# A linear-attention kernel: keys are turned before the scores, and the context products follow the scores directly

## What is computed

```python
qkv = x @ Wqkv + bqkv
xn = x / max(norm(x), 1e-12)                  # each head of q and of k
feat = exp(clip(proj(xn) * sqrt_2s - s, -20, 20)) * weights
kv_cur = cumsum(k_ch * v_ch, axis=2) + kv_state   # a chunk of 128
k_cur = cumsum(k_ch, axis=2) + k_state
ctx = einsum('bhtf,bhtfd->bhtd', q_ch, kv_cur)
den = maximum(einsum('bhtf,bhtf->bht', q_ch, k_cur), 1e-06)
out = (ctx / den) @ Wout + bout
```

## Time and profile before

| | |
|---|---|
| median of 3 runs | 1485.22 us (1483.79 to 1487.17) |
| span of the profiled execution | 1470.3 us |
| PE busy over the span | 1374.4 us (93%) |
| DVE busy | 916.3 us (62%) |
| ACT busy | 684.8 us (47%) |
| POOL busy | 551.4 us (38%) |
| attention phase in the span | 324.9 to about 774 us |

### The profile page before, as it was taken

How to read it: one execution, slowest core, us unless ns; L and a number is a source line. 1 busy time by engine, 2 the same in 40 slices (tenths; PEclk the granted TensorE clock), 3 DMA queues, 4 the chain that set the end, 5 groups by cost and what they waited for, 6 DMA issues and landing times. The chain is left out here.

```text
span 1470.3 us, 33919 instructions
## 1 busy us (share of the span) xinstructions
PE 1374.4 (93%) x12256; PEld 1193.8 (81%) x12256; DVE 916.3 (62%) x1945; ACT 684.8 (47%) x1256; POOL 551.4 (38%) x503
## 2 busy tenths in 40 slices
PE   6989999979999999999987999999699999999994
PEld 5778888867777777777766888888699999999984
DVE  4757766677787787877765164444455555555547
ACT  2456676543544544545534232322155555555543
POOL 0144555451344544444310006422334444444421
PEclk9799999989999999999997999999899999999998
DMA  6343342114223233232118004623578888888885
GB/s 233 117 141 109 124 152 100 41 35 158 73 73 129 86 100 128 82 104 100 42 42 300 8 29 159 259 103 125 171 175 241 238 235 231 237 238 233 246 268 215
DMA packets 103869, 216.12 MB, mean 147 GB/s; under 512 B 18544, under 2 KB 74224, under 8 KB 96624
## 3 DMA queue, kind: packets, MB, share of 16 engines
q1 hardware_dynamic: 79552, 159.87, 33.4%
q0 software_dynamic: 23088, 54.31, 12.9%
q10 hardware_dynamic: 1152, 0.93, 0.2%
HBM read 150.23 MB, written 64.84 MB: 146 GB/s over the span
## 5 line engine op out<-in xcount | busy, mean ns | idle before, releaser
L2522 PE MATMUL ps<-e_xhl,e_whl 128*128 128x256 f32 x1872 | 249.1, 283 | 3.9 <-DVE e_xhl L2564 3.9
L2522 PEld LDWEIGHTS ps<-e_xhl,e_whl 128*128 128x128 f32 x1872 | 234.0, 190 | 4.3 <-DVE e_xhl L2560 4.3
L1965 PE MATMUL ps<-s_xhl,s_whl 128*128 128x512 f32 x672 | 169.9, 402 | 6.2 <-PEq L1079 6.2
L2347 POOL DMA_INDIRECT xs<-e_y,e_slot_id x78 | 121.8, 1561 | 90.6 <-ACT e_y L2387 71.5
L1965 PEld LDWEIGHTS ps<-s_xhl,s_whl 128*128 128x128 f32 x672 | 126.6, 194 | 32.0 <-issue 6.3
L463 POOL TENSOR_TENSOR b_hhl<-b_h,b_hhl 128x512 fp32r<-128x512 f32 x64 | 94.3, 1477 | 140.3 <-ACT b_hhl L727 118.0
L2502 PE MATMUL ps<-e_whl,e_ghl 128*128 128x256 f32 x936 | 137.7, 283 | 0.0
L2611 DVE TENSOR_TENSOR e_g<-ps,e_act_h 128x256 f32<-128x256 f32 x156 | 66.2, 425 | 113.2 <-ACT e_act_h L2401 112.9
L2502 PEld LDWEIGHTS ps<-e_whl,e_ghl 128*128 128x128 f32 x936 | 120.6, 188 | 0.1
L2401 ACT ACTIVATE e_act_h<-ps 128x256 f32<-128x256 f32 x156 | 60.1, 385 | 112.1 <-PE ps L2522 111.8
L560 PE MATMUL ps<-b_w,b_hhl 128*128 128x256 f32 x768 | 105.3, 287 | 6.2 <-DVE b_turned_rows L833 5.4
(11 more groups left out here) (373 smaller groups left out, 2724.3 us busy)
## 6 DMA issues: line engine op xcount, KB each, us to landing
e_whl<-wlo SPq DMA_DIRECT2D x38, 1024.0 KB, 5.0
e_whl<-wlo SPq DMA_DIRECT2D x38, 512.0 KB, 3.7
c_eraw<-in_expert_w POOLq DMA_DIRECT2D x24, 512.0 KB, 4.8
wlo<-c_elo POOLq DMA_DIRECT2D x24, 512.0 KB, 3.0
wall<-in_expert_w SPq DMA_DIRECT2D x8, 1536.0 KB, 8.2
xg<-b_zeros POOLq DMA_DIRECT2D x13, 780.0 KB, 3.8
e_xr<-xg SPq DMA_DIRECT2D x39, 260.0 KB, 3.9
x<-rows_out SPq DMA_DIRECT2D x16, 512.0 KB, 3.2
```

The lines of the kernel that those rows point to most:

```text
L1965: mm = pe.matmul(ps[:, H + 2 * (m % 2) + w, :], whl[:, wp, e, lo:lo + P], xhl[:, k, xp, kd, :], start=q == 0, stop=q == 3 * KD - 1)
L2347: gp.indirect_dma_start(xs, bass.IndirectOffsetOnAxis(ap=slot_id[:, i, b:b + 1], axis=0), y[:, k, b, :], None, compute_op=ALU.add).then_in ...
L2522: mm = pe.matmul(ps[:, H + m, w * SLOT:(w + 1) * SLOT], whl[:, k, wp, lo:lo + P], xhl[:, k, xp, kd, :], start=q == 0, stop=q == 3 * KD - 1)
```

## The change

In each attention slot PE turns the keys first, then does the extra work of point B_, then the scores, and right behind them the context products of the older pair. `turn_keys` takes over the wait for both exponentials (`scores` keeps its own, which is then met). DVE reads out block B_ before it masks, where it masked first. ACT and POOL keep their order.

```diff
--- before.py
+++ after.py
@@ -1403,6 +1403,7 @@
                 mm.then_inc(s["score_done"], 1)
 
             def turn_keys(n, u):
+                pe.wait_ge(s["exp_done"], 2 * (n + 1))
                 wait(pe, "kr_ready", n)
                 for b in range(BATCH):
                     mm = pe.transpose(ps[:, KT, b * P:(b + 1) * P], kf[:, u % 4, b * P:(b + 1) * P], ids[:])
@@ -1448,9 +1449,10 @@
                         features(i, t)
                     x_steps(i, t, A_)
                     if pair(i, t, 1) is not None:
-                        scores(*pair(i, t, 1))
                         turn_keys(*pair(i, t, 1))
                     x_steps(i, t, B_)
+                    if pair(i, t, 1) is not None:
+                        scores(*pair(i, t, 1))
                     if pair(i, t, 2) is not None:
                         context(i, *pair(i, t, 2))
                     x_steps(i, t, C_)
@@ -1700,9 +1702,9 @@
                         norm_newton(norm, False)
                     if isinstance(i, int) and i == 0 and t == 1:
                         ve.wait_ge(s["weights_in"], WEIGHTS)
+                    x_evac(i, t, B_)
                     if pair(i, t, 1) is not None:
                         mask(*pair(i, t, 1))
-                    x_evac(i, t, B_)
                     if pair(i, t, 2) is not None:
                         new_state(*pair(i, t, 2))
                     if front and t == 5:
```

## The result

The changed kernel takes 1493.39 us (median of 5 runs, 1489.94 to 1501.08), the kernel before 1485.22 (5 runs, 1483.57 to 1487.17): a ratio of 1.0066, with a 95% interval of 1.0042 to 1.0091. It is slower by more than this measurement is uncertain, and 2.4 us above the top of the range given. The profiled execution took 1501.08 us with a span of 1499.5, so 1.6 us lie around a span. It was the longest of the five.

The account below looks back on a forecast made before the run. PE was taken as the bound, busy 53.59 of 55.66 us a turn. Five turns at +0.45 us (2.25), less 0.3 in turn 1, plus 0.1 in the last, made +2.1: 1487.3 us, range 1483.5 to 1491.

Parts of the forecast that it names:

- Slot 7 gains nothing: Slot 7: the scores' 0.50 us mask wait goes, but the next features wait 0.88 + 0.5 instead of 0.88.
- the edits with one answer: Every slot: the added wait in turn_keys costs nothing; keys directly behind transposes save about 0.1 us against scores there.
- Slots 0 and 1, +0.20: The late mask delays slot 0's clip and read-out, then slot 1's scores; the context moves from 9.08 to 9.28 us.
- From that context to the first FQ block the chain is as it was, so each moves by 0.20: Slots 2 and 3: everything shifts equally, the FT read-out from 20.03 to 20.23 us, FQ 0 to 20.98.
- Rival 3: The moved mask of slot 7 is held by POOL's addition; about 12 us over seven turns, 1499 us; chance 0.04.
- FQ 1 and the scores: Slot 3: FQ 1 waits for BO 3's read-out behind the moved mask; the turn's cost becomes 0.45 us.
- Slots 4 to 7, and keys behind transposes: Slots 4 to 7 carry the 0.45 us on, adding nothing; keys' saving, about 0.3 in dense turns, is otherwise swallowed by waits.
- The junction: Scores directly before context products, a pair no trace row showed: taken as 1.10 us, with ends of +-2.9 us in all.
- rivals 2 and 4: Rival 2: scores-context junction dearer, 1488.2 to 1490.2 us, chance 0.18; rival 4: cheaper, or no FQ wait, 1484.4 to 1486.2, 0.08.
- Turn 1: First loop turn: no row statistics, so slot 0's clip stands 1.3 us earlier, nothing waits, and it gains 0.3 us.
- The sum: Whole attention phase: 2.25 - 0.3 + 0.1 = +2.1 us, five turns costing 0.45 each; median 1487.3 us.
- 14.9 us around the span: Whole kernel: the median of the runs, 1485.22 us, was read as 14.9 us longer than the profiled span, 1470.3.

Follow-up runs that it names:

- x1: The changed kernel once more, unaltered: 1493.09 us against 1488.78 for the kernel before, ratio 1.0025.
- x5: The changed kernel with the 6 feature matmuls of slots 3 and 7 issued twice: 1491.32 us against 1485.38 for the kernel before, ratio 1.0042.
- x6: The changed kernel with POOL's subtraction beside the row chain cut to 8 of 1024 columns, in all turns but the first: 1484.77 us, ratio 1.0002.
- x7: The changed kernel with DVE's new order (mask behind the read-out) in slot 2 alone: 1481.69 us, ratio 0.9969 to the kernel before.
- x2: The changed kernel with PE's new order but DVE's old one (mask first): 1485.99 us, ratio 0.9973 to the kernel before.
- x3: The changed kernel with DVE's new order but PE's old one: 1496.07 us, ratio 1.0050 to the kernel before.

## Why the prediction was wrong

It said +2.1 us and "same"; measured are +8.2 in the first runs and about +3.7 and +6 in x1 and x5 (1.0025 and 1.0042). The phase is 5.6 us longer in both traces of x1 and x5. That alone would put the median at 1490.8 us, still inside the range; what took the first runs the rest of the way isn't shown. The lower clock, the end of the last turn and the holes elsewhere may each have a share. Step by step, against the full-clock turn of x1, from its start at 544.26:

- **Slot 7 gains nothing: right.** It is 6.85 us in both. The features of slot 0 wait 1.02, and the keys 0.39 for the key rows, 1.41 in sum, where 1.4 was expected of the features alone. The keys' wait for `kr_ready` was overlooked among the edits with one answer; it costs nothing, since it comes out of the wait behind it.
- **Slots 0 and 1, +0.20: right, nearly to the hundredth.** The clip of slot 0 stands at 2.43 (2.43 expected), the read-out of `FN` 3 at 6.21 (6.21), the mask at 6.81 (6.82), the first block of slot 1 at 6.95 (7.04), the scores at 8.17 (8.18), the context at 9.27 (9.28).
- **"From that context to the first FQ block the chain is as it was, so each moves by 0.20": this is the step that failed.** The `FT` read-out stands at 21.09, not 20.23, and FQ 0 at 21.84, not 20.98: 1.06 later than before instead of 0.20. The row chain does start 0.18 later (14.65 against 14.47), as said, but its first operation takes 1.29 us instead of 0.40. Only PE's timeline was moved by 0.20. DVE's clip of slot 1 moved by 1.93 (8.97 against 7.04), since a late read-out and a mask stand ahead of it, and with it moved ACT's exponentials, the expert copy behind them (12.33 against 11.23) and POOL's subtraction, from 12.44 to 13.54. It now ends at 15.92, 1.27 behind the start of the row chain. So the term "the chain is as it was", put at 0.20, measured 1.06. That x6 takes the 0.9 away by POOL's length alone shows it.
- **A question on POOL was asked about the wrong instruction.** Rival 3 asked whether the moved mask meets POOL; it isn't held, as said (1.21 us at 544.05, while POOL's addition runs from 543.33 to 545.71). The Trainium skill (SBUF — State Buffer, "SBUF: two separate sides") says that a VectorE operation with two SBUF inputs and a GpSimd operation that reads SBUF exclude each other for a whole instruction, whichever starts first. The first operation of the row chain, a tensor-tensor of two parts of `c_stats`, is such a one; the mask, which reads its other input from PSUM, is not. By that rule, the traces agree: in the loop's turns and the one behind them, in every trace but x6's, POOL starts first and this operation ends 0.01 to 0.03 us after POOL's, whatever its length between 0.30 and 1.31.
- **FQ 1 and the scores: right.** From FQ 0 to the context of slot 3 4.84 us against 4.92 expected; x7 has 4.83. The wait of FQ 1 behind the late mask formed: it follows FQ 0 after 2.15, in x2, with the old order on DVE, after 1.86.
- **Slots 4 to 7, and keys behind transposes:** the saving is real, some 0.15 a slot in most slots of x2, and isn't swallowed in slots 4 and 5; slots 4 to 7 together are 0.16 shorter in x5. The junction is 1.09 to 1.10, as taken, so rivals 2 and 4 fall. Turn 1 gains 0.8 instead of 0.3.
- **The sum.** A turn came out 1.06 longer (x1; 1.08 in x5) where 0.45 was forecast: 0.86 more up to FQ 0, 0.08 less from there to the context, and 0.16 less in slots 4 to 7. Over the whole phase it is +5.6 us in x1, with two slots at the lower clock behind the first turn, and +5.7 in x5, with none but with the doubled features.
- **The clock wasn't thought of.** PE's 0.84 us wait ahead of FQ 0, and 0.91 and 0.39 in slot 7, stand ahead of the slots that fall to the lower level. In the first trace that adds 1.2 us to slot 3 in three turns. No trace or run shows what it adds to a median. A like kernel without such slots measured no faster (x5).
- **"14.9 us around the span" was wrong.** It is 1.6. The profiled execution of before was some 13 us shorter than the median (1470.3 and 1.6 against 1485.22), and had none of the holes in the shared-expert phase. It did no harm to a difference of two spans, but a span was set against a median of other executions.

## What to carry to other kernels

When an instruction is moved on one in-order engine, follow the shift on every engine behind it and not on the critical one alone: here PE moved by 0.2 us while the chain DVE, ACT, POOL moved by 1.1, and it was POOL that struck. Ask of each VectorE operation with two SBUF inputs, the short ones above all, which long GpSimd operation stands next to it and by how much they miss each other. And where an engine waits for a chain, shorten the chain: one word in the table of slots gave 0.8%, more than all reordering around the wait.

## What the runs showed of the hardware that was not expected

- A VectorE operation on 128x4 elements with two SBUF inputs lasts 0.15 us alone and until the end of a 2.4 us GpSimd tensor-tensor operation when it starts beside it: 0.40, 0.67, 1.20, 1.29 and 1.31 us.
- It goes both ways. A 128x1024 subtraction of VectorE took 1.22 us when it started first and 3.40 when GpSimd's addition had started 0.05 earlier; that addition took 2.35 to 2.40 us without such a neighbour and 3.05 to 3.44 when it came second.
- The granted clock fell in slots that follow PE waits of 0.4 to 0.9 us in a stream otherwise full, in some executions of a kernel and not in others (slot 3 at 8.97 or 10.2 us), and behind the first turn in no slot of x3, with a wait of 0.57 in slot 1, or of x5.
- In the matmuls of the shared expert PE had 8 to 18 holes of up to 2.0 us that end by no semaphore, in all eight traces of two chips and in none of the four of two others; of the first two traces, whose chip isn't on record, one has 9 and one none. A phase with them is 8 to 22 us longer than the 284.3 of before, more than the change under study. Their cause stays open; nothing was tried on it.
